# Routed experts on tokens sorted by group: 19 tiles of 512 slots in place of 32 experts over all tokens

## What is computed

```python
x1 = einsum('bct,bcd->bdt', x, cond_weights[condition])       # 4096 tokens x 256
scores = sigmoid(x1 @ gate_w.T);  sb = scores + gate_bias     # 32 experts in 4 groups of 8
gidx = top2 of (sum of the two best sb in each group)         # two groups per token
topi = top8 of sb within these two groups
cw = 2.5 * scores[topi] / sum(scores[topi])                   # 0 for all other experts
x_lat = x1 @ fc1_w.T                                          # 128 columns
h = relu(x_lat @ w1[e].T)**2 * cw[:, e]                       # per expert e, 128 x 128
routed = (sum over e of h @ w2[e].T) @ fc2_w.T
shared = relu(x1 @ up.T)**2 @ down.T                          # inner width 512
out = x + shared + routed
```

## Time and profile before

| | |
|---|---|
| three runs, us | 527.87, 529.80, 531.67 |
| span of the profiled execution, us | 526.2 |
| median of the runs less that span, us | 3.6 |
| PE busy, us (share) | 506.9 (96%) |
| DVE busy | 409.7 (78%) |
| ACT busy | 371.0 (71%) |
| POOL busy | 118.3 (22%) |
| moved by DMA | 83.37 MB, mean 158 GB/s |

### The profile page before, as it was taken

How to read it: one execution, slowest core, us unless ns; L and a number is a source line. 1 busy time by engine, 2 the same in 40 slices (tenths; PEclk the granted TensorE clock), 3 DMA queues, 4 the chain that set the end, 5 groups by cost and what they waited for, 6 DMA issues and landing times.

```text
span 526.2 us, 8694 instructions
## 1 busy us (share of the span) xinstructions
PE 506.9 (96%) x2558; PEld 430.6 (82%) x2558; DVE 409.7 (78%) x468; ACT 371.0 (71%) x495; POOL 118.3 (22%) x143
## 2 busy tenths in 40 slices
PE   4899999999999999999999989999999999999995
PEld 4788999788888888888888879978888888888874
DVE  1237954889899898988874696599899898988985
ACT  2247775788887878878754647478887878878780
POOL 4000000124243332423200000024243332423310
PEclk9899999999999999999999999999999999999998
DMA  6990007955555555555222001745555655555614
GB/s 164 283 236 1 2 6 198 344 209 191 186 188 197 199 197 189 182 197 190 81 70 90 2 0 22 241 154 192 192 182 197 199 193 199 178 197 189 200 41 161
DMA packets 42432, 83.37 MB, mean 158 GB/s; under 512 B 7168, under 2 KB 25520, under 8 KB 42416
## 3 DMA queue, kind: packets, MB, share of 16 engines
q1 hardware_dynamic: 42224, 82.62, 47.8%
q0 software_dynamic: 192, 0.54, 0.4%
HBM read 77.91 MB, written 5.24 MB: 158 GB/s over the span
## 4 chain that ended last, share of the span: by engine, by line
PE 90%; DVE 5%; DMA 2%; ACT 1%; issue 0%; SPq 0%; DVEq 0%
PE h_banks L553 33%; PE y_banks L566 33%; PE y_banks L514 8%; PE h_banks L488 6%; PE h_banks L440 2%; PE y_banks L464 2%; PE y_banks L470 2%; PE y_banks L418 1%; DMA scale_ring<-in_cond_w,cond_sb 1%; DVE act_lo L851 1%; PE y_banks L601 1%; DVE x_res L874 1%; DMA act_full<-in_gate_w 1%; PE y_banks L382 0%; DVE scale_ring L954 0%; DVE act_lo L866 0%
## 5 line engine op out<-in xcount | busy, mean ns | idle before, releaser
L358 POOL TENSOR_TENSOR w_ring<-experts_w,w_ring 128x128 fp32r<-128x128 f32 x128 | 112.5, 900 | 386.4 <-ACT w_ring L736 386.4
L851 DVE TENSOR_TENSOR act_lo<-act_full,act_hi 128x1024 fp32r<-128x1024 f32 x144 | 182.6, 1269 | 12.3 <-ACT act_full L711 9.9
L716 ACT ACTIVATE act_hi<-scaled 128x1024 fp32r<-128x1024 f32 x128 | 136.0, 1063 | 73.8 <-PE y_banks L566 43.4
L844 DVE SCALAR_TENSOR_TENSOR scaled<-h_banks,scale_ring 128x1024 f32<-128x1024 f32 x128 | 156.7, 1224 | 36.8 <-PE h_banks L553 31.4
L553 PE MATMUL h_banks<-lat_hi,w_ring 128*128 128x512 f32 x512 | 157.8, 389 | 0.0
L566 PE MATMUL y_banks<-act_hi,w_ring 128*128 128x512 f32 x512 | 137.3, 390 | 0.0
L719 ACT ACTIVATE act_full<-scaled 128x1024 f32<-128x1024 f32 x128 | 133.6, 1044 | 0.0
L566 PEld LDWEIGHTS y_banks<-act_hi,w_ring 128*128 128x128 f32 x512 | 95.8, 188 | 20.5 <-DVE x_res L860 0.7
L553 PEld LDWEIGHTS h_banks<-lat_hi,w_ring 128*128 128x128 f32 x512 | 95.9, 188 | 19.8
L553 PE MATMUL h_banks<-lat_lo,w_ring 128*128 128x512 f32 x256 | 99.6, 389 | 0.0
L566 PE MATMUL y_banks<-act_lo,w_ring 128*128 128x512 f32 x256 | 79.4, 391 | 0.9 <-DVE act_lo L851 0.9
(11 more groups left out here) (111 smaller groups left out, 424.5 us busy)
## 6 DMA issues: line engine op xcount, KB each, us to landing
scale_ring<-s_dram SPq DMA_DIRECT2D x128, 512.0 KB, 3.8
x_in<-in_x SPq DMA_DIRECT2D x8, 512.0 KB, 5.2
experts_w<-in_w SPq DMA_DIRECT2D x8, 512.0 KB, 7.9
out_x<-x_res SPq DMA_DIRECT2D x4, 512.0 KB, 2.9
out_x<-x_res SPq DMA_DIRECT2D x8, 256.0 KB, 3.2
scaled<-in_up_w SPq DMA_DIRECT2D x1, 512.0 KB, 4.1
scaled<-in_down_w SPq DMA_DIRECT2D x1, 512.0 KB, 5.1
cond_dram<-scale_ring SPq DMA_DIRECT2D x2, 256.0 KB, 4.9
```

Of the source, the lines that this page charges most:

```text
L358: pool.tensor_tensor(ring[:, slot, 1, :], experts_w[:, w, bass.ds(e, 1), :].rearrange("q a i -> q (a i)"), ring[:, slot, 0, :].bitcast(f32 ...
L716: act.activation(act_hi[:, half, :], scaled[:, half, :], ACT.Square).then_inc(act_hi_ready, 1)
L844: dve.scalar_tensor_tensor(scaled[:, half, :], h_banks[:, half, :], 0.0, scale_ring[:, scale_slot, :], ALU.max, ALU.mult).then_inc(scaled_ ...
L851: dve.tensor_tensor(act_lo[:, slot, :], act_full[:, slot, :], act_hi[:, slot, :].bitcast(f32), ALU.subtract).then_inc(act_lo_ready, 1)
```

## The change

The two passes become one. The first phase (projection, gate and latent, shared block) runs over all eight blocks of 512 tokens, 16 shared units in all; the shared result plus x is stored to the output at once (`store_shared`). Routing runs in four batches of 1024 tokens. For each batch VectorE also finds, with TensorE's prefix sums over tokens (`rank`), in which slot of its two groups' regions each token goes. GpSimd writes each token's row of 164 numbers (128 latent, and for each group eight scales and the token's number) twice into `rows_dram`, at the slots of its two groups: 16 indirect DMAs of 128 rows per batch (`scatter`), 64 in all. `payload`, from which they are sent, has two buffers; ScalarE's `latent_and_scores` of blocks 4 and 6 waits for all scatters of batch 0 and 1.

The expert weights are split once: ScalarE and VectorE write hi and lo parts group by group, and SP stores them to `w_dram`. From the counts of the groups VectorE computes a table (`tile_table`): for each of 19 tiles its first row, its group, and whether its weights have to be loaded (1 where tile i-2 had another group; the ring has two buffers of 2 MB). Group regions are padded to a multiple of 512 slots with rows whose scales are zero and whose token number points behind the output.

Then each of the 19 tiles (i) takes four units (u) of two experts by 512 slots: rows loaded and transposed (`transpose_x`), the eight scales per slot transposed (`transpose_s`), copied, stored to `s_dram` and loaded again by broadcast (`load_scale`, four of 512 KB per tile), up, scale, squares, rest and down as before. Each tile is projected with fc2 and copied to `res`, and GpSimd adds it to the output in DRAM by four indirect DMAs with an add, 128 rows of 1 KB each, at the token numbers in `sid_sb`. The adds of one tile are issued only when those of the tile before have landed. Some matrices are laid out on the host in other order, so the 24 transposes of weights at the start are gone.

The diff, cut to its core (the new first phase and routing are told above):

```diff
+SLOTS = TOKENS * TOP_GROUPS
+X_TILES = SLOTS // BANK + GROUPS - 1
...
+            def read_table(i):
+                row_of.append(sp.value_load(table[0:1, T_ROW + i:T_ROW + i + 1], min_val=0, max_val=DUMMY))
+                col_of.append(sp.value_load(table[0:1, T_COL + i:T_COL + i + 1], min_val=LAT,
+                                            max_val=ROW - PER_GROUP))
+            def load_rows(i):
+                read_table(i)
+                if i >= 2:
+                    sp.wait_ge(x_transposed, i - 1)
+                src = rows_dram[bass.ds(row_of[i], BANK), 0:LAT].rearrange("(p j) l -> p j l", j=BT)
+                sp.dma_start(rows_sb[:, i % 2, :, :], src).then_inc(rows_loaded[i % 2], DMA)
+                if i >= 4:
+                    sp.wait_ge(out_added, (i - 3) * BT * DMA)
+                src = rows_dram[bass.ds(row_of[i], BANK), bass.ds(col_of[i], PER_GROUP)]
+                sp.dma_start(sid_sb[:, i % 4, :, :].bitcast(f32), src.rearrange("(p j) c -> p j c", j=BT))\
+                    .then_inc(sid_loaded[i % 4], DMA)
+            def load_weights(i):
+                group = sp.value_load(table[0:1, T_GROUP + i:T_GROUP + i + 1], min_val=0, max_val=GROUPS - 1)
+                need = sp.value_load(table[0:1, T_NEED + i:T_NEED + i + 1], min_val=0, max_val=1)
+                if i >= 2:
+                    sp.wait_ge(experts_done, (i - 1) * PAIRS)
+                for w, loaded in enumerate((w1_loaded, w2_loaded)):
+                    sp.dma_start(w_ring[:, i % 2, w].bitcast(f32), w_dram[bass.ds(group, 1), :, w].rearrange("a p h c -> (a p) h c"),
+                                 cond=need).then_inc(loaded[i % 2], DMA)
+            def store_s(i):
+                sp.wait_ge(s_t_copied, i + 1)
+                sp.dma_start(s_dram[i % 3], s_t[:, i % 2, :]).then_inc(s_stored, DMA)
...
+            def load_scale(i, u):
+                if i > 0:
+                    sp.wait_ge(scaled_ready, PAIRS * (i - 1) + u + 1)
+                src = s_dram[i % 3, 2 * u:2 * u + 2, :].rearrange("e t -> (e t)").rearrange("(a n) -> a n", a=1)
+                sp.dma_start(scale_ring[:, u, :], src.to_broadcast([P, UNIT])).then_inc(scale_loaded[u], DMA)
...
+            for i in range(X_TILES):
+                if i + 2 < X_TILES:
+                    load_rows(i + 2)
+                if i > 0 and i + 1 < X_TILES:
+                    load_weights(i + 1)
+                for u in range(PAIRS):
+                    if i + 1 < X_TILES:
+                        if u == 0:
+                            sp.wait_ge(s_stored, (i + 2) * DMA)
+                        load_scale(i + 1, u)
+                if i + 2 < X_TILES:
+                    store_s(i + 2)
+            sp.wait_ge(out_added, X_TILES * BT * DMA)
...
+            def scatter(k):
+                pool.wait_ge(ids_ready, k + 1)
+                pool.wait_ge(lat_copied, 2 * k + 2)
+                pool.wait_ge(s_ready, k + 1)
+                pool.wait_ge(idx_ready, k + 1)
+                for n in range(NB):
+                    for which in range(TOP_GROUPS):
+                        pool.indirect_dma_start(
+                            rows_dram, bass.IndirectOffsetOnAxis(ap=slot_idx[:, k % 2, which, n:n + 1], axis=0),
+                            payload[:, k % 2, n, :], None).then_inc(rows_scattered, DMA)
...
+            for i in range(X_TILES):
+                pool.wait_ge(sid_loaded[i % 4], (i // 4 + 1) * DMA)
+                if i > 0:
+                    pool.wait_ge(out_added, i * BT * DMA)
+                for j in range(BT):
+                    if j % 2 == 0:
+                        pool.wait_ge(res_ready, 2 * i + j // 2 + 1)
+                    pool.indirect_dma_start(
+                        out, bass.IndirectOffsetOnAxis(ap=sid_sb[:, i % 4, j, GROUP_SIZE:PER_GROUP], axis=0),
+                        res[:, i % 2, j * H:(j + 1) * H], None, compute_op=ALU.add).then_inc(out_added, DMA)
...
+            def experts_down(i, u):
+                unit = unit_of(i, u)
+                if u == 0:
+                    pe.wait_ge(w2_loaded[i % 2], (i // 2 + 1) * DMA)
+                    if i >= 2:
+                        pe.wait_ge(y_hi_ready, i - 1)
+                        pe.wait_ge(y_lo_ready, i - 1)
+                    else:
+                        pe.wait_ge(shared_added, BLOCKS)
                 pe.wait_ge(act_hi_ready, unit + 1)
-                terms = three(w2_ring[:, slot, 0], w2_ring[:, slot, 1], act_hi[:, half, :], act_lo[:, half, :])
-                for n, (w, v) in enumerate(terms):
+                y = y_banks[:, (i % 2) * BANK:(i % 2 + 1) * BANK]
+                for n in range(3):
                     if n == 2:
                         pe.wait_ge(act_lo_ready, unit + 1)
                     for m in range(2):
-                        last = pe.matmul(y_banks[:, half, m * BANK:(m + 1) * BANK], w, v[:, m * BANK:(m + 1) * BANK],
-                                         start=first_expert and n == 0, stop=last_expert and n == 2)
+                        e = slice((2 * u + m) * P, (2 * u + m + 1) * P)
+                        w = w_ring[:, i % 2, 1, 1 if n == 1 else 0, e]
+                        v = (act_lo if n == 2 else act_hi)[:, u % 2, m * BANK:(m + 1) * BANK]
+                        last = pe.matmul(y, w, v, start=u == 0 and n == 0 and m == 0,
+                                         stop=u == PAIRS - 1 and n == 2 and m == 1)
                 last.then_inc(experts_done, 1)
...
+            def ahead(i, u):
+                return divmod(PAIRS * i + u + 2, PAIRS)
+            for i in range(X_TILES):
+                for u in range(PAIRS):
+                    if ahead(i, u)[0] < X_TILES:
+                        experts_up(*ahead(i, u))
+                    experts_down(i, u)
+                    if u == 0 and i + 1 < X_TILES:
+                        transpose_x(i + 1)
+                    if u % 2 == 1 and i > 0:
+                        fc2(i - 1, u // 2)
+                    if u == 2 and i + 2 < X_TILES:
+                        transpose_s(i + 2)
+            for part in range(2):
+                fc2(X_TILES - 1, part)
...
+            def copy_res(i, part):
+                act.wait_ge(fc2_done, 2 * i + part + 1)
+                if i >= 2 and part == 0:
+                    act.wait_ge(out_added, (i - 1) * BT * DMA)
+                act.activation(res[:, i % 2, part * BANK:(part + 1) * BANK], t_banks[:, 1, :], ACT.Copy)\
+                    .then_inc(res_ready, 1)
...
+            for i in range(X_TILES):
+                relu_and_scale(i, 2)
+                rest(unit_of(i, 1))
+                if i > 0:
+                    rest_of_y(i - 1)
+                relu_and_scale(i, 3)
+                if i + 1 < X_TILES:
+                    rest_of_x(i + 1)
+                rest(unit_of(i, 2))
+                if i + 1 < X_TILES:
+                    relu_and_scale(i + 1, 0)
+                rest(unit_of(i, 3))
+                if i + 1 < X_TILES:
+                    relu_and_scale(i + 1, 1)
+                    rest(unit_of(i + 1, 0))
+            rest_of_y(X_TILES - 1)
```

More of the change, by code:

```diff
@@ L361, in _ @@
[L361 to L369 removed]
+            pool.affine_select(out=tri[:, :], in_=tri[:, :], compare_op=ALU.is_ge, fill=1.0, base=0,
+                               pattern=[[-1, P]], channel_multiplier=1).then_inc(consts_ready, 1)
```

1428 lines of the change are left out of this document (799 added, 629 removed).

## The result

The changed kernel took 610.9 us (median of 4 runs, 609.8 to 615.6), the kernel before 529.7 in the same comparison: a ratio of 1.156, 95% interval 1.151 to 1.162. I had forecast 508, range 455 to 565, with a chance of 0.32 for slower. The profiled execution has a span of 608.4 us against the 504 of my sum: 104 us are to be found.

What follows compares the result with a forecast made beforehand. Matmul time bounded the old kernel; SP's queue would pace the new tiles. First phase and turn 181, tiles 285, weights 29 and tail 9 make 504 us of span, plus 3.6 outside it: 508 us, range 455 to 565.

Steps and rivals of the forecast that it cites:

- The mechanism of the loop: Tile loop: SP's queue sets the pace through a ten-term chain, 15.0 us per tile against 13.2 of PE work.
- 1.2 for the first: Tile loop: GpSimd's issue of the first of two accumulating indirect DMAs in the chain takes 1.2 us.
- Issue 0.5 ... two table reads 0.5 each: Tile loop, SP's queue: issuing the id load takes 0.5 us and two table reads 0.5 us each.
- 3.8 to land: Tile loop: the scales of tile i+1 land 3.8 us after SP's load.
- my softest term: Tile loop: the second accumulating DMA lands 3.5 us after issue, with no such DMA in the trace.
- my own sign: First phase: experts start at 181 us; a start beyond 200 would refute the forecast of this phase.
- The later batches meet their buffers in time: First phase: only block 4 waits for a payload buffer, losing 10 us; later batches lose nothing there.
- The turn: Between first phase and experts: a strict sequence with PE idle, 17 us, including 4.5 for table reads and row loads.
- C: Rival, chance 0.22: indirect DMA issue costs 2.0 us, by waiting out VectorE's subtraction or 128 rows costing twice 64; 564 us.
- D: Rival, chance 0.14: scales, rows, adds and weights share 16 engines, so scales land in 5.2 us, not 3.8; 535 us.
- the 485: Sum if an add of 128 KB lands in a general DMA rule's 2.3 us, giving a 13.8 us loop.
- My bound of 20 us per tile: Tile loop: the length per tile with every upper bound taken, left outside the forecast range.

Runs made afterwards that it cites:

- the one with eight id buffers: Changed kernel with eight id buffers instead of four, so SP waits for the adds of tile i-6, not i-2: 528.5 us, ratio 0.996.
- The repairs together: Changed kernel with seven id and three payload buffers, earlier weight splitting, later block 7 projection, first rows before weights, tile 0's scales before tile 1's weights: 506.0 us.

## Why the prediction was wrong

I forecast 508 us and faster; it took 610.9 and was slower, outside the range.

**What bounded before, and what was removed:** right. The matmuls did become fewer, and with the wait gone PE is busy for 425.4 us, 81.5 under the 506.9 of the earlier trace rows. My terms come to less, 131 for the first phase, 251 for the tiles and a few for the tail; half a microsecond per tile (13.7 for 13.2) is 10 us of the difference, and the rest, with a mean clock of 0.91 in that kernel, I did not take apart.

**The mechanism of the loop:** right, down to the order of the steps. **Its size was the failed step,** in three terms. They come to 3.6 us, and the ring of the tile shown is 3.7 longer than my 15.0. "1.2 for the first" add: 1.63 and a gap of 0.30, 1.93. I had no accumulating DMA in the trace and took the price of plain ones; for those 1.2 was near (0.97 + 0.30 in the median of the 64 scatters). "Issue 0.5 ... two table reads 0.5 each": from 282.80 to 285.49, 2.7 us and not 1.5; SP also runs through a skipped weight transfer and its register work, which I had counted as nothing. "3.8 to land" for the scales: 5.5 to the first scaling (issue 285.49, DVE at 291.01), and 7.4 in the median of 76 where the earlier trace rows has 3.8. The landing of an add, which I called my softest term, was right: 3.9 against 3.5.

**What the ring did to PE was not in the sum at all.** I let the late wait hit only DVE's scales. But the weights' signal, also of skipped weights, stands in the same list, so PE stopped before the up projection and restarted at half clock (2.69 us for six matmuls, 1.36 in the earlier trace rows). Without SP's wait this wait of PE is gone too, and PE's busy time is 19.7 us less.

**Weights:** 4.8 per reload forecast, 5.3 measured (23.5 against 18.2 for the others on average, without the last three).

**The first phase** failed as well, by my own sign: experts started at 229.6, beyond 200. Scatters of batch 0 from 61.3 (57 forecast), landed 83.9 (79), and the hole is where I put it, but 16.5 us deep on ScalarE instead of 10. "The later batches meet their buffers in time" holds; what I left out is other: PE waits 1.4 us for block 7's x, whose buffer must be stored and loaded first, ScalarE waits 20.2 us for raw expert weights, and PE runs at a clock of 0.80 and 0.72 in the first and last window. Batch 3's scatters began at 168.1, not 144. How these share the 24 us was not taken apart. **The turn:** "4.5" for table reads and row loads left out the pads ahead of them and the 4 MB of weights: from the last scatter issue at 188.5 to the row transposes at 217.5 it took 29. The repairs together moved the first add by 18 us, from 252.3 to 234.0; the other 30 of the late start are read from the trace, and no run shows them.

**Rivals.** None alone was the result. C's sign, a busy time over 1.6 us for one indirect DMA, did not come: 1.55 for the adds (1.86 with the gap) and 0.97 for the scatters, on which almost half of its price rested. Nor is the add dear for either of C's reasons: the same 128 rows without the add took 0.97. Yet its first reason exists, on a small scale. This issue of a scatter began while VectorE ran a subtraction of two operands in SBUF:

```profile
63.84 1.22 DVE L921 TENSOR_TENSOR act_lo<-act_full,act_hi 128x1024 fp32r<-128x1024 f32 x1
```

```profile
63.94 1.98 POOL L448 DMA_INDIRECT rows_dram<-payload,slot_idx  x1 [0.30 <-issue]
```

It took 1.01 us longer than the median. At 0.1 us into the issue, the subtraction had 1.02 us left. All 13 lengthened issues of this kernel, and all 26 of the one with eight id buffers, began in this way beside L921 or L935, and wherever a single subtraction ran, the delay is what it had left, within 0.05 us. The 32 adds of the latter kernel that began beside VectorE operations that read PSUM (L1135, L1140, L1145) were not lengthened. Nor were the three issues that began less than 0.1 us before such a subtraction. In the changed kernel this is 6.0 us of scatters and 1.4 of adds, so it was not what C needed. D (scales land late) held, at 7.4 instead of its 5.2. The late landing, the dear add, SP's reads and the start together are outside the range. I also called 18 of the 19 tiles full or nearly so; by my own counts 14 are full and four hold 215 to 297 of 512 slots, with the same instructions as a full tile. And the 485 that I set beside a landing of 2.3 us is a time; as a span it is 481.

My bound of 20 us per tile contained the loop (18.9 on average with the weights); I had left it out of the range as if the ten terms erred independently, but several of them were too low at once, by one crowded queue as I read it. I had also priced the wait at 1.8 us per tile, 34 in all; without it the kernel needs 528.5, so it was worth 82.

## What to carry to other kernels

If one instruction stream feeds several consumers, a wait in it holds up every later item, also the signal of a transfer that is skipped; count what stands behind the wait for each engine, and give the buffer behind it enough depth before touching the order. A ring of steps that exceeds the compute time only slightly is no near tie, as the gaps that it opens can also cost clock, as they did here. After a wait is removed, read again: here the adds' landing doubled, since the loads that had been late now run beside them.

## What the runs showed of the hardware

- An indirect DMA of 128 rows takes GpSimd 0.97 us to issue if plain and 1.55 if it accumulates, with 0.30 between two. One that begins while VectorE subtracts two operands in SBUF takes longer by what is left of that subtraction, up to 1.0 us (39 cases in two kernels, each within 0.05 us where one subtraction ran). This is read from the times; no run varies it.
- An accumulating DMA of 128 KB lands 3.9 us after issue in the median at a DMA share of 0.7 and 7.9 at 0.9; a plain one 3.0, and 3.4 at 0.78.
- After an idle stretch of 2.4 us, with the granted clock at 1.00 before it, PE was granted 0.50: six matmuls of 512 columns took 2.69 us instead of 1.36 to 1.48.
- A conditional transfer that is skipped still signals, here when its queue reached it (SP at 284.93, the waiting PE at 285.25). Reading two table values and passing a skipped pair of transfers costs SP 1.95 us (283.54 to 285.49), far above the 48 ns of a register operation in the earlier trace rows.
